# Depthwise 5x5 convolution on TensorE: tap matrices with rows 18 floats apart, and a first channel prepared by another engine

## The reference

```python
k = jnp.transpose(kernel, (1, 2, 0))[:, :, None, :]
y = lax.conv_general_dilated(x, k, window_strides=(1, 1), padding='SAME',
        dimension_numbers=('NHWC', 'HWIO', 'NHWC'), feature_group_count=96)
return x + y
```

## Time and profile before

| | |
|---|---|
| median of 3 runs | 805.77 us |
| the profiled execution's own time | 805.91 us |
| its span in the trace | 804.1 us |
| PE busy | 790.0 us (98%) |
| DVE busy | 740.4 us (92%) |
| ACT busy | 669.6 us (83%) |
| POOL busy | 551.1 us (69%) |
| moved by DMA | 304.42 MB, mean 379 GB/s |

### The profile page before, as it was taken

The page is one execution under the profiler, slowest core; times in us unless marked ns, Lnnn a source line. Parts: engine busy times, 40 slices in busy tenths (PEclk is TensorE's granted clock), DMA queues, the critical chain, the costliest instruction groups (busy, mean ns, idle before and its releaser), DMA issues.

```text
span 804.1 us, 18943 instructions
## 1 busy us (share of the span) xinstructions
PE 790.0 (98%) x6528; PEld 788.7 (98%) x6528; DVE 740.4 (92%) x2116; ACT 669.6 (83%) x1538; POOL 551.1 (69%) x652
## 2 busy tenths in 40 slices
PE   5999999999999999999999999999999999999997
PEld 5999999999999999999999999999999999999997
DVE  5999999999999999999999999999999999999996
ACT  6788888888888888888888888888888888888885
POOL 7758668586676776766858667586676775866851
PEclk9999999999999999999999999999999999999999
DMA  9999999999999999999999999999999999999975
GB/s 359 424 407 379 405 379 370 380 398 379 397 366 377 398 373 400 364 404 367 396 364 398 379 382 378 376 391 379 398 372 403 368 392 380 371 397 379 387 294 234
DMA packets 28752, 304.42 MB, mean 379 GB/s; under 512 B 3185, under 2 KB 3313, under 8 KB 4209
## 3 DMA queue, kind: packets, MB, share of 16 engines
q1 hardware_dynamic: 28656, 303.22, 97.3%
HBM read 153.79 MB, written 149.42 MB: 377 GB/s over the span
## 4 chain that ended last, share of the span: by engine, by line
PE 96%; DVE 2%; POOL 1%; DMA 0%; issue 0%; ACT 0%; DVEq 0%; ACTq 0%
PE sums L385 32%; PE sums L392 28%; PE sums L391 27%; PE sums L388 9%; DVE x_low L330 1%; DVE y_out L341 1%; DMA first<-consts 0%; POOL matrix L284 0%; POOL spread L271 0%; ACT y_out L313 0%; ACT x_high L306 0%; POOL taps L262 0%; POOL spare L259 0%; POOL taps L257 0%; DVEq L144 0%
## 5 line engine op out<-in xcount | busy, mean ns | idle before, releaser
L385 PE MATMUL sums<-matrix,x_low 126*128 126x208 f32 (+5 forms) x2304 | 641.1, 278 | 9.3 <-POOL matrix L284 8.1
L392 PE MATMUL sums<-matrix,x_high 126*128 126x208 f32 (+4 forms) x1920 | 542.3, 282 | 0.0
L391 PE MATMUL sums<-matrix,x_high 126*128 126x208 f32 (+4 forms) x1920 | 540.8, 282 | 0.0
L284 POOL TENSOR_TENSOR matrix<-spread,mask 127x300 fp32r<-127x300 f32 x384 | 382.6, 1027 | 223.2 <-PE sums L392 221.3
L313 ACT ACTIVATE y_out<-sums 128x270 f32<-128x270 f32 (+6 forms) x1152 | 429.6, 392 | 121.2 <-PE sums L392 108.0
L385 PEld LDWEIGHTS sums<-matrix,x_low 126*128 126x128 f32 (+1 forms) x2304 | 443.8, 193 | 9.8 <-POOL matrix L284 8.1
L341 DVE TENSOR_TENSOR y_out<-sums,y_out 128x176 f32<-128x176 f32 (+2 forms) x1728 | 401.3, 275 | 52.9 <-ACT y_out L313 25.2
L330 DVE TENSOR_TENSOR x_low<-x_in,x_high 128x768 fp32r<-128x768 f32 x384 | 401.5, 1046 | 6.0 <-ACT x_high L306 6.0
L392 PEld LDWEIGHTS sums<-matrix,x_high 126*128 126x128 f32 (+1 forms) x1920 | 370.4, 193 | 0.0
L391 PEld LDWEIGHTS sums<-matrix,x_high 126*128 126x128 f32 (+1 forms) x1920 | 369.7, 193 | 0.6
L306 ACT ACTIVATE x_high<-x_in 128x768 fp32r<-128x768 f32 x384 | 321.0, 836 | 8.0 <-DMA x_in<-x 8.0
(11 more groups left out here) (5 smaller groups left out, 0.6 us busy)
## 6 DMA issues: line engine op xcount, KB each, us to landing
x_in<-x SPq DMA_DIRECT2D x95, 1536.0 KB, 10.0
y<-y_out SPq DMA_DIRECT2D x95, 1520.0 KB, 12.7
rest<-later SPq DMA_DIRECT2D x1, 2300.0 KB, 14.2
x_in<-x SPq DMA_DIRECT2D x4, 384.0 KB, 5.2
y<-y_out SPq DMA_DIRECT2D x1, 832.5 KB, 3.4
y<-y_out SPq DMA_DIRECT2D x1, 687.5 KB, 5.0
mask<-masks SPq DMA_DIRECT2D x1, 300.0 KB, 4.1
first<-consts SPq DMA_DIRECT2D x1, 125.0 KB, 2.1
```

Source lines behind the costliest of these rows:

```text
L284: pool.tensor_tensor(matrix[c % SLOTS][kind][0:whole, part, :].rearrange("p (b e) -> p b e", b=ROWS // TAPS), spread[kind][0:whole, part, ...
L385: pe.matmul(target, low, turned[:, HIGH], start=tile is bank["tiles"][0], stop=False, skip_group_check=True)
L391: pe.matmul(target, high, turned[:, LOW], start=False, stop=False, skip_group_check=True)
L392: product = pe.matmul(target, high, turned[:, HIGH], start=False, stop=last, skip_group_check=True)
```

## The change

Four things change. The rows of the tap matrix lie 18 floats apart instead of 20 (`COLS` 18; the spread taps keep rows of 20, `SPREAD`), so the mask and each part of a matrix have 270 floats instead of 300. The FLAT matrix of channel 0 is made by DVE from the constants, ahead of everything else that DVE splits or adds; POOL makes only TALL for channel 0. The masks come in two DMAs, FLAT ahead of the first input piece and TALL behind it. The first two tiles (256 of 3072 columns) of channel 0 are loaded alone on ACT's queue and split alone, and PE starts bank 0 on them; the first piece loses those columns.

```diff
-ROWS, COLS = 15, 20
+ROWS, COLS = 15, 18
+SPREAD = 20
+LEAD_COLS = PER_BANK * IMAGES
 # SP
             sp.dma_start(first[:, :], consts[:, :]).then_inc(consts_loaded, 16)
+            sp.dma_start(mask[:, FLAT, :], masks[:, FLAT, :]).then_inc(masks_loaded[FLAT], 16)
...
                 if piece == 0:
-                    sp.dma_start(mask[:, :, :], masks[:, :, :]).then_inc(masks_loaded, 16)
+                    sp.dma_start(mask[:, TALL, :], masks[:, TALL, :]).then_inc(masks_loaded[TALL], 16)
 # POOL, make_matrix
-                for kind in range(KINDS):
-                    shape = [whole, ROWS // TAPS, TAPS * COLS]
+                for kind in range(KINDS) if c else (TALL,):
+                    shape = [whole, ROWS // TAPS, TAPS, COLS]
                     for part in (HIGH, LOW):
                         pool.tensor_tensor(
-                            matrix[c % SLOTS][kind][0:whole, part, :].rearrange("p (b e) -> p b e", b=ROWS // TAPS),
-                            spread[kind][0:whole, part, :].unsqueeze(1).broadcast_to(shape),
+                            matrix[c % SLOTS][kind][0:whole, part, :].rearrange("p (b d q) -> p b d q", d=TAPS, q=COLS),
+                            spread[kind][0:whole, part, :].rearrange("p (d q) -> p d q", q=SPREAD)[:, :, 0:COLS]
+                            .unsqueeze(1).broadcast_to(shape),
...
 # ACT
+            lead = slice(0, LEAD_COLS)
+            act.dma_start(x_in[0][:, lead], x[0, :, lead]).then_inc(lead_loaded, 16)
             act.wait_ge(warm_zeroed, 1)
             act.activation(warm[:, :], warm[:, :], ACT.Copy).then_inc(warmed, 1)
+            act.wait_ge(lead_loaded, 16)
+            act.activation(x_high[0][:, lead], x_in[0][:, lead], ACT.Copy).then_inc(lead_high, 1)
 # DVE
+            def make_lead_matrix():
+                dve.wait_ge(consts_loaded, 16)
...
+                dve.tensor_tensor(high, source, centre, ALU.add).then_inc(lead_step, 1)
+                dve.wait_ge(lead_step, 1)
+                dve.tensor_tensor(lead_spare[0:whole, :, :], high.bitcast(F32), centre,
+                                  ALU.subtract).then_inc(lead_step, 1)
+                dve.wait_ge(lead_step, 2)
+                dve.tensor_tensor(low, source, lead_spare[0:whole, :, :], ALU.subtract).then_inc(lead_step, 1)
+                dve.wait_ge(lead_step, 3)
...
+                dve.tensor_copy(
+                    lead_spread[0:whole, :, :].rearrange("p h (d a e) -> p (h d) a e", d=TAPS, e=TAPS),
+                    rows.unsqueeze(2).broadcast_to([whole, 2 * TAPS, SPREAD // TAPS, TAPS])).then_inc(lead_step, 1)
+                dve.wait_ge(masks_loaded[FLAT], 16)
+                dve.wait_ge(lead_step, 4)
...
+                for part in (HIGH, LOW):
+                    dve.tensor_tensor(
+                        matrix[0][FLAT][0:whole, part, :].rearrange("p (b d q) -> p b d q", d=TAPS, q=COLS),
+                        lead_spread[0:whole, part, :].rearrange("p (d q) -> p d q", q=SPREAD)[:, :, 0:COLS]
+                        .unsqueeze(1).broadcast_to(shape),
...
+            make_lead_matrix()
+            dve.wait_ge(lead_high, 1)
+            dve.tensor_tensor(x_low[0][:, lead], x_in[0][:, lead], x_high[0][:, lead].bitcast(F32),
+                              ALU.subtract).then_inc(lead_low, 1)
             for piece in range(PIECES):
                 split_low(0, piece)
 # PE
-                    if t % (BANK_COUNT // PIECES) == 0:
+                    if c == 0 and t == 0:
+                        pe.wait_ge(lead_step, 6)
+                        pe.wait_ge(lead_low, 1)
+                    elif c == 0 and t == 1:
+                        pe.wait_ge(low_ready, 1)
+                    elif t % (BANK_COUNT // PIECES) == 0:
```

More of the change, by code:

```diff
@@ L160, in build @@
         spare = sbuf("spare", [P, GROUP, KINDS, FILTER], F32)
-        spread = [sbuf(f"spread{k}", [P, 2, TAPS * COLS], F32) for k in range(KINDS)]
+        spread = [sbuf(f"spread{k}", [P, 2, TAPS * SPREAD], F32) for k in range(KINDS)]
+        lead_taps = sbuf("lead_taps", [P, KINDS, 2, FILTER], F32R)
+        lead_spare = sbuf("lead_spare", [P, KINDS, FILTER], F32)
+        lead_spread = sbuf("lead_spread", [P, 2, TAPS * SPREAD], F32)
         warm = sbuf("warm", [P, 1], F32)
@@ L166, in build @@
         centre = first[0:whole, GROUP * TURNED:CONSTS].rearrange("p (k f) -> p k f", f=FILTER)
[L168 to L169 removed]
+        consts_loaded, later_loaded, warm_zeroed, warmed, pads_zeroed = (
+            sem(n) for n in ("consts_loaded", "later_loaded", "warm_zeroed", "warmed", "pads_zeroed"))
         first_loaded = [sem(f"first_loaded{i}") for i in range(PIECES - 1)]
@@ L174, in build, with piece_cols @@
         high_ready, low_ready = sem("high_ready"), sem("low_ready")
+        masks_loaded = [sem(f"masks_loaded{k}") for k in range(KINDS)]
+        lead_loaded, lead_high, lead_low, lead_step = (
+            sem(n) for n in ("lead_loaded", "lead_high", "lead_low", "lead_step"))
         sums_done, copied, added = sem("sums_done"), sem("copied"), sem("added")
-        def piece_cols(piece):
-            return slice(piece * PIECE_COLS, (piece + 1) * PIECE_COLS)
+        def piece_cols(piece, c):
+            return slice(max(piece * PIECE_COLS, LEAD_COLS if c == 0 else 0), (piece + 1) * PIECE_COLS)
         def plane_of(c, t):
@@ L218, in _ @@
             sp.dma_start(first[:, :], consts[:, :]).then_inc(consts_loaded, 16)
+            sp.dma_start(mask[:, FLAT, :], masks[:, FLAT, :]).then_inc(masks_loaded[FLAT], 16)
             for piece in range(PIECES):
-                cols = piece_cols(piece)
+                cols = piece_cols(piece, 0)
                 loaded = first_loaded[piece] if piece < PIECES - 1 else x_loaded[0]
@@ L266, in spread_taps @@
                 if c:
-                    pool.wait_ge(matrix_step, 2 * KINDS * c)
+                    pool.wait_ge(matrix_step, 2 * KINDS * c - 2)
                 for kind in range(KINDS):
-                    shape = [whole, 2 * TAPS, COLS // TAPS, TAPS]
+                    shape = [whole, 2 * TAPS, SPREAD // TAPS, TAPS]
                     rows = taps[0:whole, c % GROUP, kind, :, :].bitcast(F32).rearrange("p h (d e) -> p (h d) e", e=TAPS)
@@ L298, in split_high @@
             def split_high(c, piece):
-                cols = piece_cols(piece)
+                cols = piece_cols(piece, c)
                 if c == 0 and piece < PIECES - 1:
@@ L341, in add_seams @@
                     dve.tensor_tensor(y, terms, y, ALU.add).then_inc(added, 1)
+            def make_lead_matrix():
+                dve.wait_ge(consts_loaded, 16)
+                source = first[0:whole, 0:TURNED].rearrange("p (k f) -> p k f", f=FILTER)
+                high, low = lead_taps[0:whole, :, HIGH, :], lead_taps[0:whole, :, LOW, :]
+                dve.tensor_tensor(high, source, centre, ALU.add).then_inc(lead_step, 1)
[5 more added lines that the diff above has]
+                dve.wait_ge(lead_step, 3)
+                rows = lead_taps[0:whole, FLAT, :, :].bitcast(F32).rearrange("p h (d e) -> p (h d) e", e=TAPS)
+                dve.tensor_copy(
[3 more added lines that the diff above has]
+                dve.wait_ge(lead_step, 4)
+                shape = [whole, ROWS // TAPS, TAPS, COLS]
+                for part in (HIGH, LOW):
[3 more added lines that the diff above has]
+                        .unsqueeze(1).broadcast_to(shape),
+                        mask[0:whole, FLAT, :].rearrange("p (b d q) -> p b d q", d=TAPS, q=COLS),
+                        ALU.mult).then_inc(lead_step, 1)
             dve.memset(warm[:, :], 0.0).then_inc(warm_zeroed, 1)
```

8 lines of the change are left out of this document (5 added, 3 removed).

## The result

The changed kernel took 786.24 us (median of 4 runs, 784.78 to 788.4), the kernel before 805.86 beside it: a ratio of 0.9758, 95% interval 0.9735 to 0.9781. It is faster by 2.4%; 797 us, 1.1% faster, was forecast. The profiled execution took 788.4 (span 786.6).

The account below looks back on a forecast made before the run. The prediction took PE to bound the kernel, with DVE next and holding the period after the change. From 805.9 us it took 6.6 for the period and 1.9 for the start: 797 us, range 775 to 834.

Parts of the forecast that it names:

- PE's period: PE's time per channel without waits: pitch 18 takes it from 8.203 to 7.9 us, 27.6 us over 91 channels.
- columns' rule: Rival for PE's matmuls: columns set the time, so pitch gains nothing; period 8.2, 804 or 806 us; chance 0.14.
- POOL: POOL's matrix instructions: 0.72 us each at 270 floats, from 0.80; not on the path except through DVE.
- DVE's loop: DVE's time per channel: 7.53 plus 0.43 collision is 7.96, 8.58 with a tap split; 8.12 average, so DVE holds the period.
- lost race: Rival: POOL starts before DVE's third `x_low` in every channel; 8.53 us per channel, 834 us; chance 0.28.
- PE kept the bound: Rival: DVE gets ahead, its collisions stay rare and PE sets the period; 776 us; chance 0.20.
- DVE's bound: The forecast's own case: DVE sets the period, race mostly won, 785 to 804 us; chance 0.38.
- The start: Channel 0 onward: first matmul at 5.1 instead of 8.06; gain 1.9 us of 0 to 2.8, limited by channel 2.
- The sum: Whole kernel: 805.9 less 6.6 for the period and 1.9 for the start, 797.4 us; 797 predicted, 1.1% faster.
- The prediction's range: Whole kernel: 775 to 834 us, said to take in PE's bound with its 7.84 and the lost race.

Follow-up runs that it names:

- e1: The kernel before with only the pitch of 18: one mask DMA, POOL makes all matrices, no lead on DVE and ACT; 785.49 us.
- e2: The changed kernel with rows 20 floats apart again; lead, DVE's matrix and split masks stay; 806.68 us.
- e4: The kernel before with rows 22 floats apart (spread rows of 25, matrices of 330), no lead; period 8.15 us.
- e10: e7 with one memset of 96 columns on VectorE at the end of each channel; 45 us slower than e7.
- e3: The changed kernel with four y_out slots instead of three; 779.36 us.
- e5: The changed kernel, three y slots, with GpSimd building the matrices of channels 0 and 1 alone, reused by all later channels; 778.83 us.
- e7: The kernel before with rows 18 floats apart, four y slots, later channels' taps loaded behind channels 2 and 3, no lead; 776.52 us.
- e6: e3 with two more memsets of one column on VectorE at the end of each channel; time up by 3.1 us.
- e8: The changed kernel, but GpSimd begins with the taps only when VectorE has made its lead matrix; 785.87 us in one run.
- e9: The kernel before with rows 18 floats apart and four y slots, nothing else; 779.64 us.

## Why the prediction was right or wrong

*PE's period: right.* 7.9 was forecast, 7.907 is what a channel without waits takes. By kind: 13x18 0.33 forecast, 0.34 measured; 13x16 0.33 to 0.34 against 0.33 and 0.34; corners, as before on average, 0.30 in both. The count of groups predicted pitch 22 as well (8.12 expected, 8.147 the median channel). The columns' rule (the Trainium skill, "TensorE: Matmul & The Clock Gate", section "Back-to-back issue gap", which gives it for an isolated gap) would have had all pitches alike. It does not hold here: the median channels of e1, e2 and e4 take 7.907, 8.203 and 8.147 for the same columns.

*POOL: right, and no matter.* 0.72 per matrix instruction was taken; the shortest in the trace of after took 0.70, of before 0.82.

*DVE's loop: the step that failed.* The term was 7.53 + 0.43 = 7.96, "already over PE's 7.9", and 8.58 for the channel with a tap split: 8.12 on average. The 7.53 was right. The collision of the fourth `x_low` costs 1.23 - 0.95 = 0.28, not 0.43: I had scaled the 0.49 of the earlier trace rows with POOL's instruction, but what DVE waits for is the rest of the instruction then running. POOL's instruction at that moment, before (fourth `x_low` at 38.45) and after (at 267.42):

```profile
38.24 0.83 POOL L284 TENSOR_TENSOR matrix<-spread,mask 127x300 fp32r<-127x300 f32 x1
```
```profile
267.11 0.73 POOL L297 TENSOR_TENSOR matrix<-spread,mask 127x270 fp32r<-127x270 f32 x1
```

The rest was 0.62 before (38.45 to 39.07) and cost 0.49; it was 0.42 after (267.42 to 267.84) and cost 0.28. The cost is the rest less 0.13 or 0.14, and so it is for the lost race of e10: a rest of 0.66 (329.24 to 329.90) and 0.53. In each of the twelve traces the median over all `x_low` that start inside a matrix instruction of POOL is the rest less 0.13. The fourth `x_low` now meets a later part of POOL's sequence. That makes 7.80 (third `x_low` to third, 36.47 to 44.26 in the trace of after, 234.31 to 242.11 in e3). In the channel with a split it is 8.16: the split makes POOL's matrix late too (257.95, 0.43 behind PE's start instead of 0.31), so the third `x_low` still comes first, where I had it collide. The average is (3 x 7.80 + 8.16) / 4 = 7.89, under PE's 7.90 by 0.01, instead of 0.22 over it. It took both misses: with the fourth collision alone put right it is (3 x 7.81 + 8.43) / 4, some 7.97, still over PE's. So PE kept the bound, which I had given 0.20, with 91 x 0.22 = 20 us more than the forecast. That the measured 786.24 lies in 785 to 804, the range given to DVE's bound, is luck: it comes from PE's bound and waits that stood in no step.

*What took 9.3 of that back was in no step:* a store landed 13.2 after its issue (12.7 before), but three slots of 7.9 hold less time than three of 8.2. ACT waited for its slot, and a DVE with 0.01 of slack could not make up for it and lost the race in 13 channels: 8.7 of the 9.3 us. With the fourth slot (e3) two such channels are left. The slot's life should have been held against the store's landing, since the change shortens the one and not the other. How much of the waiting the shorter slot's life makes by itself stays open: e5, with the same slots and the same channel of 7.907, waited 11.7 and not 78.5.

*The lost race: right as a mechanism.* It wasn't the changed kernel's steady state, though 13 of its channels are of that kind; e10, with rows 18 apart and four slots, shows it 0.06 us of DVE work away: 8.39 per channel where 8.53 was priced, 821 where 834 was. The Trainium skill ("SBUF — State Buffer", section "SBUF: two separate sides") says that whichever of the two engines starts first holds the shared port pair for its whole instruction; the rows agree but for a constant: 0.06 behind POOL cost 0.53, 0.13 less than the 0.66 that POOL's instruction still ran.

*The start: wrong in both parts.* First matmul 5.1 forecast, 7.61 measured, because the constants came 0.45 later (at 3.4 to 3.6 in the kernels with the lead, at 2.8 to 3.1 in those without) and the lead's 1.7 + 0.4 became 3.14 + 0.9 beside POOL's taps. I had priced the DVE instructions alone and listed POOL's only as what DVE replaces. And 1.9 of gain was taken where nothing (e2: 0.6 lost) came: as the prediction said, channel 2 waits for its input; the rest of the start fills up that wait. e7 shows the lever, the order of the loads.

*The sum:* forecast were 6.6 from the period and 1.9 from the start. The profiled execution gained 17.5: 26.9 from PE's period (91 x 0.296) less 9.3 in waits, and about 0 from the start. The median gained 19.6; the profiled execution is the slowest of the four, 788.4 where the fastest took 784.78, and this spread is larger than the 2 us between.

*The prediction's range:* it was said to take in PE's bound with its 7.84 per channel. Worked out, 805.9 - 1.9 - 91 x 0.363 is 771, below the 775 that was given; with 7.907 nothing hangs on it.

## What to carry to other kernels

- Before asking whether an engine is faster after a change, write down the loop of every engine and its slack in the new period: here PE 7.907, DVE 7.89, a y slot's 3 x 7.9 against a store's landing. Whichever has none left turns delays of others into time; busy shares (DVE 94 and 95%) don't show it.
- Where two engines exclude each other, a loop has two lengths, by who comes first. Find who wins and by how much, and keep the margin well above the jitter: 0.06 us of work per channel cost 45 us here.
- In this kernel a float32 operand on TensorE's moving side costs by the aligned groups of four floats that its rows touch (65 groups 0.36, 59 groups 0.33 to 0.34 for three matmuls), down to a floor of 0.31 to 0.33. Choose pitch and first column so that rows share groups.
- A collision with GpSimd costs VectorE the rest of the instruction then running, less 0.13 here. So its price depends on where in that instruction it starts, and cannot be scaled from another kernel.

## What the hardware showed that I had not expected

- The start of a GpSimd instruction 0.02 us ahead of VectorE's decides nothing reliably: at the same distance VectorE once lost (1.51) and once won (0.95), both in e6.
- The kernel with the earliest first matmul came to its full pace latest. In e8 13x18 tiles took 0.66 to 0.67 up to 16.05 and 0.33 to 0.34 from 18.70 on, half the pace and the full one, as the two levels of 1.2 and 2.4 GHz stand to each other; PE began at 5.80 there and was idle for 1.25 before 11.55. An earlier start alone does not order it: e6 began at 7.09 and kept the full pace from 12.19 to 19.75, e9 began at 7.92 and had it from 14.32. One window of before (first matmul 8.06) and the same of e8 show it by the count of PE's matmuls:

```profile
12.00:14.00 2.00, 2.00 (x19) 2.00 (x18) 0.69 (x4) 1.23 (x3) 1.92 (x3) 1.00 1.03 442
```
```profile
12.00:14.00 2.00, 2.00 (x11) 2.00 (x11) 0.85 (x3) 0.70 (x1) 1.92 (x4) 1.00 1.01 432
```

  PE is busy for 2.00 in both, with 19 matmuls against 11, and the PEclk column reads 1.00 in both, so here the pace has to be read from the count. What set the later rise in e8, its pause or something else, was not tried.
- Two memsets of one column, each 0.06 busy, lengthened VectorE's loop by 0.03 together; one of 96 columns, 0.14 busy, by 0.06.
